# Layer 1: the index list one group earlier, and two VectorE operands in PSUM

## The reference, cut to what matters

```python
s_u = x @ W_u.T + b_u
s_v = x @ W_v.T
e = s_u[src] + s_v[dst]
e = jnp.where(e >= 0, e, 0.2 * e)
m = jax.ops.segment_max(e, dst, num_segments=n_nodes)
e_exp = jnp.exp(e - m[dst])
denom = jax.ops.segment_sum(e_exp, dst, num_segments=n_nodes)
probs = e_exp / denom[dst]
xh = x.reshape(n_nodes, head_dim, num_heads)
msg = xh[src] * probs[:, None, :]
out = jax.ops.segment_sum(msg, dst, num_segments=n_nodes)
```

## Time and profile before

| | |
|---|---|
| median of 3 runs | 4935.61 us (4934.03 to 4941.12) |
| profiled execution, its own time | 4929.81 us |
| its span in the profile | 4928.1 us |
| granted TensorE clock, mean | 0.80 |
| PE busy | 3099.3 us (63%) |
| DVE busy | 2202.6 us (45%) |
| ACT busy | 908.4 us (18%) |
| POOL busy | 3434.9 us (70%) |
| L1466, gathers of layer 1, POOL | 880 times, 1008.1 us busy, 605.6 us idle before them |
| L1699, product with the weights, DVE | 220 instructions, 264.0 us busy |
| L1532, sums of a pair, PE | 1760 records, 555.7 us busy |

### The profile page before, as it was taken

The page is one execution under the profiler, slowest core; times in us unless marked ns, Lnnn a source line. Parts: engine busy times, 40 slices in busy tenths (PEclk is TensorE's granted clock), DMA queues, the critical chain, the costliest instruction groups (busy, mean ns, idle before and its releaser), DMA issues. The chain is left out here.

```text
span 4928.1 us, 61408 instructions
## 1 busy us (share of the span) xinstructions
PE 3099.3 (63%) x13554; PEld 1900.6 (39%) x13555; DVE 2202.6 (45%) x5019; ACT 908.4 (18%) x2810; POOL 3434.9 (70%) x2948
## 2 busy tenths in 40 slices
PE   3547877777777777877778768834444444444441
PEld 1224444444444444444444435523333333333331
DVE  2543333333333333333333349855555555555554
ACT  0212222222222222222222223300000000000002
POOL 4238888888888888888888867756666666666564
PEclk9869898888998888888898889956666666666665
DMA  7777767667767677677677666643333333333332
GB/s 285 193 241 137 135 126 136 133 123 135 132 126 138 127 131 134 126 135 132 123 136 132 123 133 206 181 148 93 95 92 100 93 94 91 96 98 94 92 93 66
DMA packets 471760, 641.52 MB, mean 130 GB/s; under 512 B 173608, under 2 KB 365636, under 8 KB 467887
## 3 DMA queue, kind: packets, MB, share of 16 engines
q0 software_dynamic: 198144, 339.26, 36.4%
q1 hardware_dynamic: 245994, 254.83, 17.6%
q10 hardware_dynamic: 27588, 47.08, 3.0%
HBM read 448.23 MB, written 192.71 MB: 130 GB/s over the span
## 5 line engine op out<-in xcount | busy, mean ns | idle before, releaser
L935 POOL DMA_INDIRECT S<-l_msum,l_sink x784 | 1280.7, 1634 | 254.2 <-issue 213.5
L1466 POOL DMA_INDIRECT l_feats<-X_rows,l_gsrc x880 | 1008.1, 1146 | 605.6 <-DVE l_gsrc L1574 340.7
L918 POOL DMA_INDIRECT l_ga<-A_rows,l_gsrc x784 | 791.3, 1009 | 265.6 <-issue 155.4
L1008 PE MATMUL l_psU<-l_hid,l_same 128*128 128x257 f32 x1568 | 585.0, 458 | 534.7 <-ACT l_hid L1044 518.2
L981 PE MATMUL l_psC<-l_table,l_onehot 128*128 x4728 | 726.5, 295 | 0.0
L1532 PE MATMUL l_psU<-l_feats,l_same 128*128 128x264 f32 x1760 | 555.7, 481 | 146.5 <-DVE l_feats L1699 129.2
L1048 ACT COPY l_msum<-l_psU 128x257 f32<-128x257 f32 x784 | 292.6, 373 | 1883.8 <-POOLq L934 1296.1
L974 PE MATMUL l_psC<-W1cT,l_attrT 64*128 64x256 f32 x1576 | 619.0, 476 | 13.1 <-DMA l_table<-B_rows 13.1
L981 PEld LDWEIGHTS l_psC<-l_table,l_onehot 128*128 128x128 bf16 x4728 | 426.0, 104 | 364.9 <-issue 303.4
L1008 PEld LDWEIGHTS l_psU<-l_hid,l_same 128*128 128x128 f32 x1568 | 266.1, 213 | 669.9 <-ACT l_hid L1044 598.9
L1532 PEld LDWEIGHTS l_psU<-l_feats,l_same 128*128 128x128 f32 x1760 | 413.8, 242 | 281.8 <-issue 189.2
(11 more groups left out here) (346 smaller groups left out, 3512.2 us busy)
## 6 DMA issues: line engine op xcount, KB each, us to landing
l_srcb<-src_rows SPq DMA_DIRECT2D x99, 512.0 KB
l_locb<-lo_rows SPq DMA_DIRECT2D x55, 512.0 KB
S<-su_zeros ACTq DMA_DIRECT2D x24, 1156.5 KB
l_locb<-loc_rows SPq DMA_DIRECT2D x99, 256.0 KB
nd_sums<-S SPq DMA_DIRECT2D x196, 128.5 KB, 2.2
l_attr<-in_edge_attr SPq DMA_DIRECT2D x98, 256.0 KB
GH_rows<-l_hidden SPq DMA_DIRECT2D x49, 384.0 KB
nd_hidden<-GH_rows SPq DMA_DIRECT2D x49, 384.0 KB, 3.2
```

What stands on the lines that cost most here:

```text
L918: pool.indirect_dma_start(ga[:, s, :], None, D["A"], bass.IndirectOffsetOnAxis(ap=gsrc[h][:, j % HALF:j % HALF + 1], axis=0)).then_inc(gat ...
L935: pool.indirect_dma_start(D[f"S{j % NTAB}"], bass.IndirectOffsetOnAxis(ap=sink[j // HALF][:, j % HALF:j % HALF + 1], axis=0), msum[:, j % ...
L1008: nc.tensor.matmul(psU[j % 2][:, 0:UW], same[j // HALF][:, j % HALF, :], hid[:, j % RING, :], start=True, stop=True).then_inc(agg_done, 1)
L1466: pool.indirect_dma_start(feats[r][:, t, :], None, D["X1"], bass.IndirectOffsetOnAxis(ap=gsrc[r][:, t:t + 1], axis=0)).then_inc(gathered[r ...
```

## The change

The list for group g + 2 is copied as the first step of DVE's body g instead of the last. Both comparisons that build `same` read the column numbers from PSUM (copied there once), and the four products with the weights read the weights from PSUM. For that ACT writes the exponential twice: first into the new bank `psW`, which releases DVE's products, and then into `feats` as before, which PE now waits for, since the sum of the weights is taken from there. All other steps of DVE keep their order.

```diff
@@ layer1_phase
+        psW = m.ps("psW", [P, 512])
+        weights_in_rows = m.sem("weights_in_rows")
+        weight = psW[:, 0:GROUP * NH].rearrange("p (t h) -> p t h", h=NH)
+        column = psW[:, P:2 * P]
@@ PE's body
                 pe.wait_ge(same_ready, g + 1)
+                pe.wait_ge(weights_in_rows, g + 1)
@@ ACT's body
                 act.wait_ge(below_ready, g + 1)
-                nc.scalar.activation(feats[r][:, :, H:XW], below[:, :, :], ACT.Exp).then_inc(weights_ready, 1)
+                nc.scalar.activation(weight, below[:, :, :], ACT.Exp).then_inc(weights_ready, 1)
+                nc.scalar.activation(feats[r][:, :, H:XW], below[:, :, :], ACT.Exp).then_inc(weights_in_rows, 1)
@@ DVE's find_edge
-                nc.vector.tensor_tensor(same[:, :, :], K["column"][:, :].unsqueeze(1).to_broadcast([P, GROUP, P]),
+                nc.vector.tensor_tensor(same[:, :, :], column.unsqueeze(1).to_broadcast([P, GROUP, P]),
@@ DVE, ahead of the loop
+            nc.vector.tensor_copy(column, K["column"][:, :])
@@ DVE's body
+                if not isinstance(g, int) or g < XG - SETS:
+                    stage_index(g + SETS, r)
                 if not last:
                     find_node(g + 1, 1 - r)
...
-                    f = feats[r][:, q * QUARTER:(q + 1) * QUARTER, :]
-                    f3 = f[:, :, 0:H].rearrange("p t (c h) -> p t c h", h=NH)
-                    w3 = f[:, :, H:XW].unsqueeze(2).to_broadcast([P, QUARTER, H // NH, NH])
+                    f3 = feats[r][:, q * QUARTER:(q + 1) * QUARTER, 0:H].rearrange("p t (c h) -> p t c h", h=NH)
+                    w3 = weight[:, q * QUARTER:(q + 1) * QUARTER, :].unsqueeze(2).to_broadcast([P, QUARTER, H // NH, NH])
...
                     local_max(g + 1, 1 - r, c)
-                if not isinstance(g, int) or g < XG - SETS:
-                    stage_index(g + SETS, r)
```

More of the change, by code:

```diff
@@ L1401, in layer1_phase @@
         max_ready, max_turned = m.sem("max_ready"), m.sem("max_turned")
-        below_ready, weights_ready = m.sem("below_ready"), m.sem("weights_ready")
+        below_ready, weights_ready, weights_in_rows = m.sem("below_ready"), m.sem("weights_ready"), m.sem("weights_in_rows")
         weighted, agg_done, acc_done = m.sem("weighted"), m.sem("agg_done"), m.sem("acc_done")
```

## The result

| | before | after |
|---|---|---|
| median, 4 runs each | 4938.36 us (4934.03 to 4941.62) | 5079.09 us (5077.7 to 5082.99) |
| span of the profiled execution | 4928.1 us | 5075.9 us |
| granted TensorE clock, mean | 0.80 | 0.788 |
| POOL busy | 3434.9 us | 3276.7 us |

The ratio is 1.0287 [1.0269, 1.0305]: slower by 141 us, where 306 us less were forecast. From the scores of group 1 to those of group 54 a group now takes (4970.47 - 3289.41) / 53 = 31.72 us instead of 29.11.

A forecast was written before the change was run, and what follows sets the result against it. The bound was a circle of list, 16 gathers, landing and scores, 29.11 us a group; saving 314.7 us and spending 8.0 and 0.3 gave 4623.4, or 4629.2 us as a median, range 4570 to 4690.

The forecast's parts named there:

- The list one group earlier: List copy at the start of DVE's body: ends DVE's wait for gathered rows, 5.94 us a group, 314.7 us saved.
- POOL's waits for the sums of PE: Expected sign: POOL idles for the second or third sum of a group, 2 to 3 us each, no longer for the list.
- DVE with operands in PSUM: Compare and four products on DVE's chain: taken as 0; bounds 6 ns less each or up to 0.5 us a group more.
- POOL with operands in PSUM: Gathers beside DVE's compare and products: 3.2 us a group of POOL stalls may go; counted as nothing in the sum.
- So 8 us of slack cover the gathers: Behind the early list: the sixteenth gather's rows land at 4133.6, the scores want them at 4141.8, so DVE doesn't wait.
- POOL beside those steps: DVE's one-input steps newly beside a busy POOL may be held: 0.15 us a group, 8.0 us in all.
- The third: Rival: DVE's one-input steps wait for whole gathers, or landings come late; 26.0 us a group, 4770 us; chance 0.09.
- The fourth: Rival: PSUM operands halve DVE's rate in the compare and products; 30.5 us a group, 5008 us; chance 0.03.
- The first: Rival: POOL becomes the bound, its stalls staying though the operands moved; 23.9 us a group, 4660 us; chance 0.14.
- The fifth: Rival: the wait for rows stays, gathers held by something the gates don't show; 4930 to 4936 us; chance 0.03.
- the second: Rival: PE's clock comes up earlier as PE rests less, 1.7 us a group less; 4538 us; chance 0.07.
- A sum of the clock's part: PE's sums: a pair takes 1.73 us at the lower clock, 0.89 at the higher, 0.84 apart; no shift taken.

The follow-up runs named there:

- e1: Only the list copied one group earlier, operands left in SBUF, against the kernel before: 4716.36 us, ratio 0.9541.
- e2: Only the compare's and products' operands moved to PSUM, list still copied late, against the kernel before: 5143.79 us, ratio 1.0405.
- r1: The changed kernel, unedited, run again on another chip: 5077.24 us, ratio 1.0277 to the kernel before.
- r2: The changed kernel plus a POOL memset of about 1 us ahead of every quarter's four gathers, on a chip that holds: 4672.25 us, ratio 0.9457 to the kernel before.
- r5: The changed kernel plus POOL memsets of 0.6 us ahead of every quarter, on a chip that doesn't hold: 4582.00 us, ratio 0.9342 to the kernel before.
- r3: The changed kernel with gathers of half a row, same count, no pause, on a chip that holds: 5076.42 us, ratio 1.0275 to the kernel before.
- e7: The changed kernel with gathers of half a row, no pause, on a chip that doesn't hold: 4581.5 us, ratio 0.9353 to the kernel before.
- e8: The changed kernel plus one POOL memset of about 2 us ahead of the ninth gather, on a chip that doesn't hold: 4644.10 us, ratio 0.9481 to the kernel before.
- e6: The changed kernel plus POOL memsets of 0.2 us ahead of every quarter, on a chip that doesn't hold: 4576.84 us, ratio 0.9344 to the kernel before.

## Why the prediction was wrong

- **The list one group earlier: right.** L1594 doesn't wait for rows in the loop, and e1 alone gives 227 of the 306 us forecast. Where nothing is held, a group has 22.98 us. POOL's waits for the sums of PE came as named, but 96 of 6.5 us in the mean (625.1 in all) instead of 2 to 3 us each, since the holds lie in them.
- **DVE with operands in PSUM: right.** 1215 ns a product and 2285 a compare (3280 to 4990 us). By the Trainium skill's "VectorE: DVE Perf Modes" (its section on the TRN2 errata) a source in PSUM makes the fixed part of an instruction longer; it is not seen, with 1215 against e1's 1220 ns and e2's 2291 against 2282.
- **POOL with operands in PSUM: the step that failed.** The text said: "it is only the difference between POOL with rest and POOL as a second bound, so I count nothing for it in the sum". The gathers did fall to 0.95 us, as that step said. But POOL's stalls, counted as pure loss, kept the gathers at 1.465 us, and with them PE's signals got through (no late count in the kernel before, short ones in e1); at 1.264 DVE stands for held ones for 8.26 us a group. The term set at 0 is 31.72 - 24.82 = 6.9 us a group behind the early list (the ratios 1.0277 of r1 and 0.9541 of e1, each to the kernel before on its own chip, are 7.4% apart, some 363 us), and 32.97 - 29.11 = 3.9 behind the late one.
- **"So 8 us of slack cover the gathers": right for the rows, wrong as a statement on the gathers' cost.** It asks only when the rows land. Gathers ran beneath DVE's carries before too, but the first of a series; behind the early list it is the ninth to thirteenth, and PE answers DVE three times there. The prediction named POOL beside those steps only for their one SBUF input (0.15 us a group), and that part was small as it said: L1678 takes 273 ns in the mean where L1670 took 318.
- **A row misread.** The earlier trace rows show the scores of group 0 with 10.22 us of idleness. I used only the row of group 1 beside it. Asking what released group 0, whose rows belong to the first 16 of 32 gathers, would have led to PE's late count at 3258.55. That alone gives no size for the loop, but a reason not to set the term at 0.
- **The rivals.** The third (late steps of DVE, now that POOL never rests, 4770) had the place, DVE's steps beneath a POOL that never rests, but another mechanism (whole gathers holding DVE's one-input steps) and a third of the size, 2.8 us. The fourth ended on the right side through a rate of DVE that didn't change. The first is refuted: the stalls went with the operands. The fifth is too, since the wait for rows went, and the second isn't seen: the granted clock is 0.50 from 4101.4 to 4106.0, where the sums of a group start.
- **A sum of the clock's part** mixes two readings of the earlier trace rows: 5 matmuls with their busy time (2.16) and 9 with the length of the stretch (2.00). With 1.81, their busy time, a pair takes 0.80 us and not 0.89 at the higher level. Nothing in the forecast hung on it.
- **The range** ended at 4690, 389 us short; a rival in which the freed POOL costs more than it gives wasn't among the six cases.

**What stays open.** That rests in POOL's series are enough to bring DVE's held waits from 8.26 us a group to 0.4 is shown by r1 against r2 on one chip. What inside the chip makes PE's counts late (PE's writes, the semaphores' path, or what POOL's descriptors share with either) is not shown by any run; nor why DVE's and ACT's counts are on time, why it begins near the ninth gather, or why two chips don't do it. The length of rest that suffices between 0.2 and 1 us a quarter is open too (r5, with 0.6, fell on a chip that doesn't hold).

## What to carry to other kernels

A stall of an engine off the path can be what lets another signal through: before removing one, ask what runs longer without a break, whose signals cross it, and how far into it they fall. The first place to look is a stretch of the same trace in which that already happens, here the fill ahead of the loop, and the row whose idle time has no plausible releaser. If a wait names a load that ended long ago, look for two engines that start at the same hundredth: they wait for the same late signal. Where the trace records the semaphores' counts, set the count's time beside the end of the instruction that makes it. Measure a cure and the disease on one chip.

## What the runs showed of the hardware

- While POOL issues indirect DMAs at 1.25 us each, PE's counts of a semaphore are recorded up to 11.9 us after the product's end, once it ends beneath the ninth gather of a series or a later one (112 of 112 in the changed kernel; none of 328 beneath the first eight). DVE waits up to 9.8 us, and 49 of its 54 held waits over 1 us end 3.6 to 4.1 us after the last gather's start. DVE's and ACT's own counts are at most 35 ns behind in all twenty traces.
- With stalls or rests of POOL at a mean pace of 1.465 to 1.49 us the counts are on time (the kernel before) or, where late, some 1 us in the median (e1, r2). The late ones then fall beneath the first eight gathers too (e1: 70 of 322).
- Ahead of the loop, beneath 32 gathers, ACT's copies of 0.21 us, which wait for no other engine, have 1.19 us between them, once 3.92.
- Half the bytes in as many gathers change nothing in this (r3, 1.0275 against r1's 1.0277).
- Chips differ: on two, with the kernel before at 4896.84 and 4904.7 us, no such delay is seen in six kernels; on the others it takes 4938 to 4944 us. The same kernel with half rows takes 4581.5 us on one of the two (e7) and 5076.42 on another chip (r3).
- Two SBUF operands against one with the other in PSUM, same operation and shape: next to no difference for DVE (2282 and 2291 ns; 1220 and 1215 ns), while the mean gather falls from 1171 to 949 ns (e1 and e2, 3280 to 4600 us).
- DVE's one-hot in bf16 takes 1994 ns beside a memset of 2036 ns on POOL, against 791 beside memsets of 229 (e8 and e6).
